# Two thirds of the weight preparation dealt to tiles 1 to 24 of attention

## The reference

```
x = x + attention(layernorm(x), ctx, positions)      # 32 heads of 8, rope on q and k
z = layernorm(x)
top2 of z @ Wg.T over E = 8 experts, softmax of the two scores
x = x + sum over the chosen experts e of  share * (silu(z @ W1[e].T) * (z @ W2[e].T)) @ W3[e].T
```

## Time and profile before

| what | value |
|---|---|
| time, median of 3 runs | 539.72 us (539.54 to 542.92) |
| the profiled execution's own time | 541.64 us |
| its span, first to last instruction | 539.9 us |
| busy in the span | PE 473.8, DVE 416.0, POOL 358.6, ACT 324.5 us |
| TensorE clock granted, mean | 0.963 of full speed |

### The profile page before, as it was taken

How to read it: one execution, slowest core, us unless ns; L and a number is a source line. 1 busy time by engine, 2 the same in 40 slices (tenths; PEclk the granted TensorE clock), 3 DMA queues, 4 the chain that set the end, 5 groups by cost and what they waited for, 6 DMA issues and landing times.

```text
span 539.9 us, 21592 instructions
## 1 busy us (share of the span) xinstructions
PE 473.8 (88%) x7697; PEld 365.5 (68%) x7697; DVE 416.0 (77%) x1268; ACT 324.5 (60%) x833; POOL 358.6 (66%) x564
## 2 busy tenths in 40 slices
PE   3766999999999999999999998899999999998830
PEld 2653666666667666666766665578989999987720
DVE  7486599898999989899999988766765555469836
ACT  2473767766676676767767675546555565555410
POOL 5333658888888888888888886328785555465430
PEclk9987999999999999999999998979999999999975
DMA  7910011111212122121211101233744433368938
GB/s 206 248 32 18 19 33 38 60 54 49 63 49 83 59 69 74 49 63 39 70 44 56 41 32 36 72 101 100 214 137 137 132 119 123 121 193 276 317 124 286
DMA packets 49463, 54.48 MB, mean 101 GB/s; under 512 B 6821, under 2 KB 45135, under 8 KB 49360
## 3 DMA queue, kind: packets, MB, share of 16 engines
q1 hardware_dynamic: 42880, 36.28, 23.8%
q0 software_dynamic: 6480, 16.82, 8.4%
HBM read 29.57 MB, written 23.90 MB: 99 GB/s over the span
## 4 chain that ended last, share of the span: by engine, by line
PE 53%; DVE 27%; issue 8%; DMA 6%; ACT 3%; SPq 2%; POOL 1%; POOLq 0%; DVEq 0%; ACTq 0%
DVE negmax L730 12%; PE logit_banks L1510 10%; PE bank L1366 6%; PE logit_banks L1529 5%; PE logit_banks L1326 5%; PE qkv_banks L1275 5%; DVE ropes L715 4%; PE logit_banks L1334 4%; DMA y_in<-result_rows 3%; PE qkv_banks L1286 3%; PE qkv_banks L1266 3%; PE bank L1486 2%; DVE rden L737 2%; DMA xres<-in_L_ffn_W_dram 2%; PE qkv_banks L1316 1%
## 5 line engine op out<-in xcount | busy, mean ns | idle before, releaser
L658 POOL DMA_INDIRECT result_rows<-blocks_io,blk_dest x71 | 70.4, 991 | 64.5 <-POOL blk_dest L651 28.9
L625 POOL DMA_INDIRECT routed_rows<-xs,slots x64 | 65.9, 1030 | 16.8 <-issue 16.8
L730 DVE TENSOR_REDUCE negmax<-logit_banks 128x16 f32<-128x1024 f32 x64 | 75.0, 1213 | 2.1 <-PE logit_banks L1307 2.1
L1135 ACT ACTIVATE late<-logit_banks 128x1024 f32<-128x1024 f32 x64 | 62.0, 1021 | 15.5 <-PE logit_banks L1334 15.5
L632 POOL TENSOR_TENSOR ropes<-rope_a,ropes 128x512 f32<-128x512 f32 x32 | 41.1, 1285 | 34.7 <-DVE ropes L715 34.7
L1013 DVE TENSOR_TENSOR gated<-xn,logit_banks 128x176 f32<-128x176 f32 x71 | 23.9, 336 | 49.0 <-ACT xn L1229 42.4
L737 DVE RECIPROCAL rden<-bank 128x256 f32<-128x256 f32 x32 | 55.9, 1747 | 2.3 <-PE bank L1359 2.3
L1229 ACT ACTIVATE xn<-logit_banks 128x176 f32<-128x176 f32 x71 | 22.5, 317 | 53.6 <-PE logit_banks L1510 53.6
L1510 PE MATMUL logit_banks<-w_hi,x_hi 128*128 x142 | 47.5, 334 | 7.9 <-DVE x_lo L1024 5.9
L616 POOL TENSOR_TENSOR mid<-mid,mask 128x512 f32<-128x512 f32 x44 | 44.8, 1038 | 11.8 <-ACT mid L1116 11.8
L1510 PE MATMUL logit_banks<-w_lo,x_hi 128*128 x142 | 45.9, 323 | 0.0
(11 more groups left out here) (226 smaller groups left out, 1353.0 us busy)
## 6 DMA issues: line engine op xcount, KB each, us to landing
blocks_io<-routed_rows SPq DMA_DIRECT2D x71, 128.5 KB, 2.8
y_in<-result_rows SPq DMA_DIRECT2D x32, 256.0 KB, 4.4
x_sb<-in_x_dram SPq DMA_DIRECT2D x32, 128.0 KB, 2.1
out_dram<-o_sb SPq DMA_DIRECT2D x16, 256.0 KB, 3.9
ctx_sb<-in_ctx_dram SPq DMA_DIRECT2D x32, 64.0 KB, 2.6
blocks_io<-in_L_ffn_W_dram SPq DMA_DIRECT2D x4, 512.0 KB, 7.3
mid<-mT SPq DMA_DIRECT2D x128, 4.0 KB
routed_rows<-pad_row SPq DMA_DIRECT2D x15, 128.5 KB, 3.2
```

Source lines behind the costliest of these rows:

```text
L625: nc.gpsimd.indirect_dma_start(routed[:, :], bass.IndirectOffsetOnAxis(ap=slots[:, t.slot(TR), k:k + 1], axis=0), xs[:, t.slot(TR), k, :], ...
L658: nc.gpsimd.indirect_dma_start(results[:, :], bass.IndirectOffsetOnAxis(ap=blk_dest[:, b.slot(RB):b.slot(RB) + 1], axis=0), y_sb[:, b.slot ...
L730: V.tensor_reduce(negmax[:, t.par, 16 * half:16 * half + 16], ps_s[:, 1024 * half:1024 * half + 1024].rearrange("p (h k) -> p h k", k=N), ...
L1135: S.activation(pT[:, 1024 * half:1024 * half + 1024], ps_s[:, 1024 * half:1024 * half + 1024], ACT.Exp, scale=SCALE).then_inc(exp_done, 1)
```

## The change

The 24 steps become 32, because each W3 step is halved (one expert's first 128 rows, then the rest). Steps 0 to 7 stay where they were. The other 24 are dealt one to each turn c = 1 to 24, and all of them use PSUM bank 5. On PE the transposes come after the transposes of q and k, behind a wait for the copy of v (v_sb); on ACT the copy comes between the copy of q and k and the copy of the maxima; on DVE the subtraction comes right after the peak and before the choice of experts. PE waits for the subtraction before the projection of k, which writes bank 5 again. PE at turn -1 waits only for step 7. The raw W3 is laid out by expert, so that add_bias can wait for the step of each tile that it overwrites. The one copy of L1155 falls to turn 8.

```diff
...
         xres = sb("xres", [P, T, D])
         late_x = xres[:, XOWN:T, :].rearrange("p t d -> p (t d)")
         w12b = late_x[:, 0:E * D].rearrange("p (e d) -> p e d", e=E)
-        w3_raw = late_x[:, E * D:E * D + KC * E * (HP + H2)].rearrange("p (c e h) -> p c e h", c=KC, e=E)
+        w3_raw = late_x[:, E * D:E * D + KC * E * (HP + H2)].rearrange("p (e c h) -> p c e h", c=KC, e=E)
         exp_i = sb("exp_i", [1, NBLK], I32)
         x_sb = sb("x_sb", [P, 2, D])
         ctx_sb = sb("ctx_sb", [P, 2, CD])
...
         N_POOL_CONST, N_DVE_CONST, N_W = 10, 10, 2
         NW12 = E * KC
-        NWT = NW12 + E
+        NWT = NW12 + 2 * E
+        NFIRST = NW12 // 2
         wt_banks = [banks[0], banks[1], banks[2], banks[3]]
         ps_pos = banks[3][:, 0:2 * T]
         ps_h, ps_y, ps_hT = banks[0:2], banks[2:4], banks[4:6]
...
         y_half = rope_a[:].rearrange("p (a d) -> p a d", a=2)
+        def weight_bank(n):
+            return wt_banks[n % 4] if n < NFIRST else banks[5]
         def weight_copy(n):
-            ps = wt_banks[n % 4]
+            ps = weight_bank(n)
             if n < NW12:
                 hi = w12_hi[:, n // KC, n % KC, :]
-                return hi, ps[:, 0:2 * H], [(w12_lo[:, n // KC, n % KC, :], ps[:, 0:2 * H], hi)]
-            e = n - NW12
-            rest = w3_hi[H2:P, e, 1, :]
-            return (w3_hi[:, e].rearrange("p c d -> p (c d)"), ps[:, 0:2 * D],
-                    [(w3_lo[:, e], ps[:, 0:D], w3_hi[:, e, 0, :]), (rest, ps[H2:P, D:2 * D], rest)])
+                return hi, ps[:, 0:2 * H], w12_lo[:, n // KC, n % KC, :], ps[:, 0:2 * H], hi
+            e, rest = (n - NW12) // 2, w3_hi[H2:P, (n - NW12) // 2, 1, :]
+            if (n - NW12) % 2:
+                return w3_hi[:, e, 1, :], ps[:, 0:D], rest, ps[H2:P, 0:D], rest
+            return w3_hi[:, e, 0, :], ps[:, 0:D], w3_lo[:, e], ps[:, 0:D], w3_hi[:, e, 0, :]
+        def weight_steps(c):
+            return range(NFIRST + c - 1, NFIRST + c) if 1 <= c <= NWT - NFIRST else range(0)
         def rank_of(t):
...
             def add_bias(t):
                 pool.wait_ge(w_in, 16 * N_W)
-                if t.n == XOWN:
-                    pool.wait_ge(wt_sb, NWT)
+                if t.n >= XOWN:
+                    e = t.n - XOWN
+                    pool.wait_ge(wt_sb, 2 * e + 2 if e < E else NW12 + (e - E) // 2 * 2 + 2)
                 nc.gpsimd.tensor_tensor(xres[:, bass.ds(t.n, 1), :].rearrange("p a d -> p (a d)"),
                                         x_sb[:, t.par, :], bout_sb[:], ALU.add).then_inc(xb_done, 1)
...
                 for n in which:
                     dve.wait_ge(wt_hi, n + 1)
-                    for lo, ps, hi in weight_copy(n)[2]:
-                        ins = V.tensor_tensor(lo, ps, hi.bitcast(F32), ALU.subtract)
-                    ins.then_inc(wt_sb, 1)
+                    lo, ps, hi = weight_copy(n)[2:]
+                    V.tensor_tensor(lo, ps, hi.bitcast(F32), ALU.subtract).then_inc(wt_sb, 1)
             def body(do, t):
...
                     do(rope, t.plus(2))
                 do(mean_of_x1, t.plus(-2))
                 do(keep_gate, t.plus(2))
-                if is_first(t, 1):
-                    split_weights(range(11, NWT))
                 do(peak, t.plus(1))
+                split_weights(weight_steps(t.c))
                 do(best_scores, t.plus(-2))
                 do(best_experts, t.plus(-2))
                 do(mark_choices, t.plus(-2))
...
                 do(place_tokens, t.plus(-2))
                 do(select_places, t.plus(-2))
                 do(set_slots, t.plus(-2))
-                if is_first(t, 2):
-                    split_weights(range(8, 11))
                 if is_first(t, 3):
                     rope(tile(0))
                     split_weights(range(0, 4))
...
                         act.wait_ge(wf3_in, 16 * KC)
                         S.activation(w3_raw[:, :, :, HP:HP + H2], w3_raw[:, :, :, P:HP], ACT.Copy).then_inc(w3_twice, 1)
                     act.wait_ge(wt_done, n + 1)
-                    hi, ps, _ = weight_copy(n)
+                    hi, ps = weight_copy(n)[0:2]
                     S.activation(hi, ps, ACT.Copy).then_inc(wt_hi, 1)
             def sines():
...
                 if is_first(t, 4):
                     copy_wg()
                 do(mask_queries, t.plus(1))
-                if is_first(t, 1):
-                    copy_weights(range(11, NWT))
                 do(copy_kqT, t.plus(2))
+                copy_weights(weight_steps(t.c))
                 do(copy_mT, t.plus(1))
                 do(normalise_x1, t.plus(-2))
                 do(exponential, t, 0)
...
                     copy_weights(range(0, 2))
                     copy_gate_weights()
                     copy_weights(range(6, 8))
-                if is_first(t, 2):
-                    copy_weights(range(8, 11))
             pipeline(body)
...
                     if n == NW12:
                         pe.wait_ge(w3_twice, 1)
                     if n >= 4:
-                        pe.wait_ge(wt_sb, n - 3)
-                    ps = wt_banks[n % 4]
+                        pe.wait_ge(wt_sb, n - 3 if n < NFIRST else n)
+                    ps = weight_bank(n)
                     if n < NW12:
                         e, c = n // KC, slice(n % KC * P, n % KC * P + P)
                         M.transpose(ps[:, H - H2:3 * H - H2].rearrange("p (w h) -> p w h", w=2)[:, :, 0:H2],
...
                         M.transpose(ps[:, 0:P], w12a[:, 0, e, c], ident[:])
                         ins = M.transpose(ps[:, H:H + P], w12a[:, 1, e, c], ident[:])
                     else:
-                        e = n - NW12
+                        e, part = (n - NW12) // 2, slice(0, P) if (n - NW12) % 2 == 0 else slice(P, HP + H2)
                         for d in range(KC):
-                            M.transpose(ps[:, d * P:(d + 1) * P], w3_raw[:, d, e, 0:P], ident[:])
-                            ins = M.transpose(ps[:, D + d * P:D + (d + 1) * P],
-                                              w3_raw[:, d, e, P:HP + H2], ident[:])
+                            ins = M.transpose(ps[:, d * P:(d + 1) * P], w3_raw[:, d, e, part], ident[:])
                     ins.then_inc(wt_done, 1)
             pe.wait_ge(pool_const, N_POOL_CONST)
...
                 if is_first(t, 3):
                     pe.wait_ge(wqk_ready, KC + 2)
                 if is_first(t, 1):
-                    transpose_weights(range(8, NWT))
-                    pe.wait_ge(wt_sb, NWT)
+                    pe.wait_ge(wt_sb, NFIRST)
                 do(logits, t.plus(1))
                 do(attend, t.plus(-1), 0)
                 do(attend, t.plus(-1), 1)
                 do(transpose_kq, t.plus(2))
+                if weight_steps(t.c):
+                    pe.wait_ge(v_sb, t.n + 1)
+                transpose_weights(weight_steps(t.c))
                 do(transpose_max, t.plus(1))
                 do(shifted_logits, t)
                 do(rank, t.plus(-2))
+                if weight_steps(t.c):
+                    pe.wait_ge(wt_sb, NFIRST + t.c)
                 do(project_k, t.plus(3))
                 do(project_v, t.plus(1))
                 do(project_out, t.plus(-1))
```

## The result

The changed kernel takes **603.4 us** (599.7 to 606.6, 4 runs) against 540.9 us before (539.5 to 542.9, 4 runs): a ratio of 1.110 (95% interval 1.106 to 1.115; the ratios given here and below are not quotients of the medians shown, and differ from them by up to 0.5%). 546.6 was forecast, with a range up to 552. The profiled execution has a span of 601.7 us and a mean granted clock of 0.915; before it had 539.9 and 0.963.

What follows compares the result with a forecast made beforehand. Bounds: weight preparation alone at the start, then PE and DVE both nearly full in each 9.47 us turn. The start's -15.0 and the steps' +21.9 gave +6.9, so 546.6 us from a median of 539.72; 8-in-10 range 537 to 552.

Steps and rivals of the forecast that it cites:

- The start: Before the turns: first logits at about 27.75 us, rope of tile 2 at 33.5 to 35.6, a gain of 15.0 us.
- Nothing on PE, ACT and in the bank: In turns 1 to 24: PE's transposes, ACT's weight copy and the bank wait before the k projection cost nothing.
- DVE's wait for ACT and its work: Between peak and choice: wait about 0.9 us, subtraction 0.45 (W3 0.42), so the choice begins 1.44 us late (W3 1.33).
- The step that failed: DVE's queue behind the late choice: 0.46 us of slack is free, so a W1/W2 turn grows 0.98 us, W3 0.87.
- The clock rival: Attention turns: PE idles 1 us a turn and its clock falls, 9 us more, 556 us in all; chance 6%.
- the forecast's delay: Added by the dealt steps: turns 2 to 8 6.9 us, 9 to 24 13.9, doubling copy about 1.1; together 21.9.

Runs made afterwards that it cites:

- act_only: Changed kernel without the 24 dealt steps' PE transposes and DVE subtractions; ACT writes the same arrays by copies from finished weights: 529.3 us, ratio 0.975.
- choice_first: Changed kernel with one line moved, so that DVE's subtraction comes after the choice of experts: 531.2 us, ratio 0.978.
- mask_late: Changed kernel with POOL's mask_keys made to wait, from tile 6 on, until DVE has chosen the experts: 557.9 us, ratio 1.030.
- dose_long_apart: Kernel before, plus a 1.45 us DVE reciprocal between peak and choice in turns 1 to 24, and mask_keys waiting for the choice: 567.2 us, ratio 1.045.
- warm: Changed kernel plus dummy PE transposes in turns 2 to 24, 8 before the ranks and 5 before the output projection: 582.8 us, ratio 1.071.
- dose_short: Kernel before, plus a short DVE reciprocal (128x56, some 0.43 us planned) between peak and choice in turns 1 to 24: 564.2 us, ratio 1.034.
- early: Changed kernel with PE's transposes between attend's halves and ACT's weight copy before the q and k copy; subtraction still before the choice: 543.8 us, ratio 1.002.

## Why the prediction was wrong

**The start** was right in its steps: logits at 27.33 (forecast 27.75), rope of tile 2 at 34.58 (33.5 to 35.6), a gain of 15.4 there for 15.0. By rope of tile 3 it is 11.8 to 14.6 over the runs that have the change, for in some of them the clock stays low a turn longer than I allowed.

**Nothing on PE, ACT and in the bank**: right. act_only and choice_first show it, and PE never waits for the subtraction.

**DVE's wait for ACT and its work**: right in size. The wait was put at 0.91 and is 0.91 in the turn shown; MAX8 is late by what was forecast. With the meeting taken away, mask_late has turns of 10.4 and 10.2 to 10.5, within 0.13 of the forecast, and the 1.45 us of dose_long_apart cost 0.82 a turn.

**The step that failed** is the one that follows: "Behind it in DVE's queue are the reciprocal and the normalisation, for which PE's output projection waits". I moved the choice of experts 1.44 us back and kept its length of 0.8 us; its growth was put at nothing without a reason. It measured 1.78, and PE waits 1.02 us for it ahead of the ranks, a wait that the forecast did not follow at all. I looked at what else is queued behind a late operation on its own engine, and not at what runs on POOL at the time to which it moves. There, mask_keys holds up operations of DVE. The Trainium skill (SBUF — State Buffer, Who interferes with whom) says that a DVE instruction with two SBUF inputs contends with a GpSimd instruction that reads SBUF, and that the second to issue is blocked until the first is done. This case agrees: onehot, chosen, seen and place have two inputs in SBUF and grow (means of 540, 878, 469 and 688 ns for 174, 202, 287 and 162), while MAX8, with one input in SBUF, stays at 0.16 us beside mask_keys, and so did the reciprocal out of PSUM before, at 1.74. I had not applied it. The trace of the kernel before had shown it, too, in a turn near the end where mask_keys came early (DVE, then POOL):

```profile
328.76 1.01 DVE L777 TENSOR_TENSOR onehot<-iota_e,idx 128x16 f32<-128x16 f32 x1
329.81 0.95 DVE L783 TENSOR_TENSOR chosen<-onehot 128x8 bf16<-128x8 f32 x1
...
328.70 2.04 POOL L616 TENSOR_TENSOR mid<-mid,mask 128x512 f32<-128x512 f32 x2
```

**The clock rival** was named, at 6%, with 9 us. Its premise, one wait of PE of about 1 us in a turn, is nearly what mask_late has once its edit has begun, 0.66 to 0.78 us, and there I was nearly right: of the turns 4 to 24 two fell, 8 and 24. In the changed kernel PE idles twice, 1.02 and 0.66 us close together, and the clock falls in 17 of the turns 2 to 24. The rival's 9 us were half of what the clock cost here, 17.8.

The sum from rope of tile 3 to rope of tile 27, as the runs take it apart: the forecast's delay with few falls of the clock, +29.7 (mask_late: 257.2 less 227.5; about 5.0 of it is turns 2 and 3, where the meeting is still there, and turns 8 and 24 are together 2.6 above the forecast); the meeting with POOL, +27.1 (warm: 284.4 less 257.2); the clock, +17.8 (302.2 less 284.4); together +74.7, against 21.9 forecast. The parts hold in this order; taken away in another, their sizes would differ, since in these turns the clock falls behind the other two.

## What to carry to other kernels

When an operation moves in time, look at what every other engine does at the place where it lands, not only at who waits for it: DVE's small operations on two SBUF inputs and POOL's elementwise work beside them were worth more than all the work moved. In a loop where two engines are nearly full, put an operation with a late operand behind whatever could run while it waits; here one line moved by four stages is 72 us. And cost a new wait of PE with the clock behind it, by the stretches of the trace where such waits already stood.

## What the runs showed of the hardware

In turns 2 to 24 of the changed kernel PE waits 0.8 to 1.2 us for the choice and, in all but one, 0.4 to 0.8 for the normalisation (1.02 and 0.66 in the turn shown, 2.1 us between their ends); its granted clock fell in 17 of these 23 turns. With one wait in a turn, mostly of 0.66 to 0.78 us, it stayed at 0.98 to 1.00 in all but one or two turns of a run (mask_late, dose_short, dose_long_apart, early). 13 dummy transposes, some 1.9 us of PE time in a turn, took 20 us off the kernel. And chosen, an operation of 0.2 us on DVE, ended with the POOL operation that it met, to within 0.05 us, when that had about 0.95 us to go; so did onehot, when it had 0.43 (dose_short). They are held until the other is done, and not slowed by a factor.
